# Attention heads: TensorE's last value sums and second turned score block, issued ahead of the next head's first scores

## The chip, the cores and the metric

One core of a Trainium2 chip runs the whole program. The metric is the device time of one execution in microseconds (us). Two kernels are compared by their median times; a profiled execution gives the rows below.

## The reference

Two "macaron" layers work on 1024 tokens of width 512: half feed-forward, mixer, half feed-forward. The mixer of the first layer is a Mamba2 scan, that of the second is causal attention with 32 heads of width 16 (8 key and value heads), and this case is about those heads alone:

```python
draft = einsum('bhqd,bhkd->bhqk', qr, kr) + causal
_, draft_indices = top_k(draft, 128)          # the 128 largest scores of each row stay
scores = einsum('bhqd,bhkd->bhqk', qr, kr) / sqrt(16) + mask
out = einsum('bhqk,bhkd->bhqd', softmax(scores), v)
```

A row may look at its own and earlier tokens, and of these only at its 128 best.

## The kernel before, in words

The function attention_heads_fast (L1822) takes one head after the other. The 1024 rows of a head are 8 tiles of 128; tile t has (t + 1) x 128 columns. A head goes through four phases, each in its own round of a software pipeline, so that in round n TensorE (L2063), VectorE (L2372), ScalarE (L2123) and GpSimd (L2237) work on five heads at once:

- Head n + 1: TensorE samples the scores (L1950, for a guess of each row's 128th best), then makes the scores of each tile in PSUM (scores, L1964 and L1966). VectorE takes the row maximum of tile 0 (L2270) and copies tiles 1 to 7 into z (L2274). scores(h, t) waits until VectorE has read what lay in that half of the bank before (z_done, L1959): scores(n + 1, 0) waits for the copy of tile 7 of head n.
- Heads n and n - 1: a search for the cut. ScalarE counts the scores above a trial value (L2102, four sweeps over the tiles), VectorE counts the smallest tile of two sweeps (L2307), GpSimd moves the trial value after each sweep (move, L2174) and writes the cut (L2217).
- Head n - 2: VectorE marks what reaches the cut (take, L2283). TensorE makes the scores again with the marked ones taken out (marked_scores, L1981 to L1987), VectorE finds with MAX8 which of the rest or surplus to change (pick, L2319) and writes `picked` with MATCH_REPLACE8 (L2327, named tables or picked).
- Head n - 3: the scores are made again, turned, in 12 blocks (exponents, L2013 to L2023). A block (b, t0, t1) holds 128 key tokens against the row tiles t0 to t1: blocks 0 to 3 have 512, 384, 256 and 128 columns, blocks 4 to 8 have 512, blocks 9 to 11 have 384, 256 and 128. Each lies in one of two PSUM banks by turns (ps_e). Those with b = t0 end with the mask matmul L2023. ScalarE makes the exponential of a block (L2113) into one of three buffers, TensorE sums it with the values (add_v, L2037) into ps_oT, VectorE copies and divides the sums one round later (L2335, L2342, L2344).

exponents(h, i) waits for the exponential two blocks earlier (its bank), for the row maxima and for the picks of its tiles. add_v(g) waits for the exponential of block g. ScalarE's exponentials are spread over its sweeps by a table worked out ahead (EXP_BEFORE); the last block of a head is taken at the start of the next round (LATER = 1), block 0 and block 1 in the first sweep too.

The order of TensorE is written out by hand in tables: CHUNKS_AHEAD before the sample, CHUNKS_FIRST before tile 1, and others after the marked scores or the scores of a tile. (VALUES, -1) is the last block of the head before. The core of it:

```python
CHUNKS_AHEAD = ((SCORES, 0), (VALUES, -2))
CHUNKS_FIRST = ((VALUES, -1), (SCORES, 1), (SCORES, 2))
```

Rounds run from n = -1 to 34; n + 1 is a head up to n = 30, n - 3 from n = 3.

Of the kernel before, what the change touches and what calls it, by code (L numbers as in the profile page):

```python
# [1821 lines left out]
def attention_heads_fast(nc, env, X, qT, kT, v, mixed, q_tok, k_sums):  # L1822
# [8 lines left out]
    LAST_CHUNK = [max(i for i, (b, t0, t1) in enumerate(CHUNKS) if t0 <= t < t1) for t in range(NT)]  # L1831
    SCORES, VALUES = "scores", "values"
    CHUNKS_AHEAD = ((SCORES, 0), (VALUES, -2))
    CHUNKS_FIRST = ((VALUES, -1), (SCORES, 1), (SCORES, 2))
    CHUNKS_AFTER_MARKED = {4: ((SCORES, 6), (VALUES, 4)), 7: ((SCORES, 11), (VALUES, 9))}
    CHUNKS_AFTER_SCORES = {1: ((VALUES, 0), (SCORES, 3), (VALUES, 1)), 2: ((SCORES, 4), (VALUES, 2)), 3: ((SCORES, 5), (VALUES, 3)),
                           4: ((SCORES, 7), (VALUES, 5)), 5: ((SCORES, 8), (VALUES, 6), (SCORES, 9), (VALUES, 7)),
# [16 lines left out]
    with ExitStack() as ctx:  # L1854
# [74 lines left out]
        live = lambda h: 0 <= h < AH  # L1929
# [10 lines left out]
        def _(pe):  # L1940
            def sample(h):

                if h >= 4:
                    pe.wait_ge(rows_done, h - 3)
                if h >= 6:
                    pe.wait_ge(divided, h - 5)
                if h >= 1:
                    pe.wait_ge(stats_done, 3 * h)
                for t in range(1, NT):
                    last = pe.matmul(ps_sample[:, t - 1, :], qT[:, h, t * P:(t + 1) * P], k_sums[:, h // REP, t, :],  # L1950
                                     start=t == 1, stop=True, skip_group_check=True)
                last.then_inc(sampled, 1)

            def scores(h, t):

                L, at = (t + 1) * P, z_at(t)
                done = h * NT + t - (0 < t < 4)
                if done:
                    pe.wait_ge(z_done, done)  # L1959
                for n in range(0, L, BANK):  # L1960
                    w = min(BANK, L - n)
                    diagonal = n + w == L
                    if diagonal:
                        pe.matmul(ps_z[:, at + L - P:at + L], env.ident_bf[:], env.future_bf[:], start=True, stop=False,  # L1964
                                  skip_group_check=True)
                    last = pe.matmul(ps_z[:, at + n:at + n + w], qT[:, h, t * P:(t + 1) * P], kT[:, h // REP, n:n + w],  # L1966
                                     start=not diagonal, stop=True, skip_group_check=True)
                last.then_inc(s_done, 1)

            def marked_scores(h, t):  # L1970

                L, at = (t + 1) * P, m_at(t)
                pe.wait_ge(take_done, h * W + t)
                done = h * W + t - 1 - (1 < t < 4)
                if done:
                    pe.wait_ge(pick_done, done)
                for n in range(0, L, BANK):
                    w = min(BANK, L - n)
                    diagonal = n + w == L
                    if diagonal:  # L1980
                        pe.matmul(ps_m[:, at + L - P:at + L], env.ident_bf[:], env.future_bf[:], start=True, stop=False,  # L1981
                                  skip_group_check=True)
                    pe.matmul(ps_m[:, at + n:at + n + w], qT[:, h, t * P:(t + 1) * P], kT[:, h // REP, n:n + w],  # L1983
                              start=not diagonal, stop=False, skip_group_check=True)
                for n in range(0, L, BANK):
                    w = min(BANK, L - n)
                    last = pe.matmul(ps_m[:, at + n:at + n + w], ident_taken[:], mark[:, (h * W + t) % 2, n:n + w], start=False, stop=True,  # L1987
                                     skip_group_check=True)
                last.then_inc(marked, 1)

            def turned_rows(h):

                pe.wait_ge(split_done, h + 1)
                if h + 3 < AH:
                    pe.wait_ge(stats_done, 3 * (h + 4))
                if h:
                    pe.wait_ge(rows_done, h)
                if h >= 3:
                    pe.wait_ge(divided, h - 2)
                pe.matmul(ps_rows, parts_all[:], env.ident_bf[:], start=True, stop=True).then_inc(row_done, 1)  # L2000

            def exponents(h, i):

                b, t0, t1 = CHUNKS[i]
                g = h * NCH + i
                if g >= 2:
                    pe.wait_ge(exp_done, g - 1)
                pe.wait_ge(rows_done, h + 1)
                if g == 0:
                    pe.wait_ge(set_up, FACTORS)  # L2010
                out = ps_e[g % 2]
                pe.wait_ge(pick_done, h * W + t1 - 1)
                pe.matmul(out[:, 0:t1 - t0, :], kT[:, h // REP, b * P:(b + 1) * P], qT[:, h, t0 * P:t1 * P],  # L2013
                          start=True, stop=False, skip_group_check=True)
                for t in range(t0, t1):
                    if t:
                        at = OFF[t] + b * P
                        pe.matmul(out[:, t - t0, :], picked[:, h % 2, at:at + P], ident_back[:], start=False, stop=False,  # L2018
                                  skip_group_check=True)
                    last = pe.matmul(out[:, t - t0, :], minus_rows[:, t, :], rows[:, h % 2], start=False, stop=True,  # L2020
                                     skip_group_check=True)
                if t0 == b:
                    last = pe.matmul(out[:, 0, :], env.future_bf[:], env.ident_bf[:], start=False, stop=True,  # L2023
                                     skip_group_check=True)
                last.then_inc(et_done, 1)

            def add_v(g):

                h, i = divmod(g, NCH)
                b, t0, t1 = CHUNKS[i]  # L2030
                v_at = (b * KVH + h // REP) * (AD + 1)
                pe.wait_ge(exp_done, g + 1)
                if i == 0 and h:
                    pe.wait_ge(kept_o, h)
                for t in range(t0, t1):
                    at = 2 * AD * (t % 4)
                    last = pe.matmul(ps_oT[at:at + 2 * AD, t // 4, :], env.v_all[:, v_at:v_at + 2 * AD], eT[:, g % 3, (t - t0) * P:(t - t0 + 1) * P],  # L2037
                                     start=b == 0, stop=b == t, skip_group_check=True)
                last.then_inc(av_done, 1)

            def turn_out(h):

                pe.wait_ge(kept_o, h + 1)
                if h == 0:
                    pe.wait_ge(set_up, FACTORS)
                else:
                    pe.wait_ge(divided, h)
                pe.wait_ge(rows_done, min(h + 3, AH))
                for half in range(2):
                    last = pe.matmul(ps_o[:, 4 * half:4 * half + 4, :], o_kept[:, half, :], untwist[:], start=True, stop=True,  # L2050
                                     skip_group_check=True)
                last.then_inc(o_turned, 1)

            def turn_and_add(h, steps):

                for kind, i in steps:
                    if kind == SCORES:
                        exponents(h, i)
                    elif h * NCH + i >= 0:
                        add_v(h * NCH + i)  # L2060

            pe.wait_ge(set_up, SET_UP)
            for n in range(FIRST, LAST):  # L2063
                if live(n - 3):
                    turn_and_add(n - 3, CHUNKS_AHEAD)
                if live(n + 1):
                    sample(n + 1)
                    scores(n + 1, 0)
                if live(n - 3):
                    turn_and_add(n - 3, CHUNKS_FIRST)  # L2070
                for t in range(1, NT):
                    if live(n - 2):
                        marked_scores(n - 2, t)
                        if t == ROWS_TURNED:
                            turned_rows(n - 2)
                    if live(n - 4) and t == OUT_TURNED:
                        turn_out(n - 4)
                    if live(n - 3):
                        turn_and_add(n - 3, CHUNKS_AFTER_MARKED.get(t, ()))
                    if live(n + 1):  # L2080
                        scores(n + 1, t)
                    if live(n - 3):
                        turn_and_add(n - 3, CHUNKS_AFTER_SCORES.get(t, ()))
# [455 lines left out]
```

## Time and profile before

| | |
|---|---|
| median of 3 runs | 3132.11 us (3128.52 to 3133.68) |
| profiled execution | 3127.38 us, its span 3125.6 us |
| attention heads | from 2064 to about 3004 us of the span |
| busy over the span | TensorE 89%, VectorE 80%, ScalarE 61%, GpSimd 52% |

Times in the rows are us from the start of the span. In a timeline a row has start, duration, engine, line, operation, tile written <- tile read, and in brackets how long the engine had been idle and what ended it. PE is TensorE, DVE VectorE, ACT ScalarE, POOL GpSimd. A TensorE row's duration covers the whole way of the data through the array, and the next matmul starts before it ends, so the step from start to start is what a matmul costs. Several tiles share memory and carry an older name: X is the memory of the exponentials and marks, tables that of `picked`.

### The profile page before, as it was taken

The numbers are of one execution on the slowest core, as the hardware profiler recorded it, in microseconds if no ns is written. First come the engines' busy times: TensorE is split into PE (matmuls) and PEld (weight loads), VectorE is DVE, ScalarE is ACT, GpSimd is POOL, SyncE is SP. The second block draws the span as 40 slices with busy tenths as digits, with TensorE's granted clock in tenths as the row PEclk, the third lists the DMA queues.
The fourth block names the chain that finished last, engine by engine and source line by source line (L and its number), as shares of the span: only waits on it lengthen the run. The fifth ranks groups of instructions, "written<-read, shape, count | busy, mean of one in ns | idle before, by whom it ended". The sixth has DMA issues, their size and how long they took to land. (4 is left out here: it accounts for less than half of the span.)

```text
span 3125.6 us, 50560 instructions
## 1 busy us (share of the span) xinstructions
PE 2780.4 (89%) x15833; PEld 1523.0 (49%) x15833; DVE 2494.2 (80%) x4792; ACT 1919.3 (61%) x4058; POOL 1640.1 (52%) x3595
## 2 busy tenths in 40 slices
PE   8899999999999999999999989856777777777769
PEld 4455455455455454454554554533444444444444
DVE  5678687697697696796796887768999999999846
ACT  2464554554564554554554543369999999999823
POOL 3236245255264263263362354568777787777603
PEclk9999999999999999999999999967999999998989
DMA  2223122132132242132232220000000000000010
GB/s 91 62 77 105 68 91 91 68 102 81 68 110 70 74 119 87 56 114 78 71 108 72 70 90 21 28 1 1 2 2 2 2 2 2 2 2 2 1 52 28
DMA packets 65804, 169.62 MB, mean 54 GB/s; under 512 B 11776, under 2 KB 19328, under 8 KB 64512
## 3 DMA queue, kind: packets, MB, share of 16 engines
q1 hardware_dynamic: 54448, 115.17, 11.7%
q10 hardware_dynamic: 11088, 51.19, 4.7%
q8 instruction: 131, 2.15, 0.3%
q14 instruction: 137, 1.12, 0.1%
HBM read 161.08 MB, written 5.24 MB: 53 GB/s over the span
## 5 line engine op out<-in xcount | busy, mean ns | idle before, releaser
L2102 ACT ACTIVATE X<-ah_z,ah_trial 128x512 bf16<-128x512 f32 (+6 forms) x832 | 703.9, 857 | 21.6 <-POOL ah_trial L2212 11.6
L1207 ACT ACTIVATE m_mix<-m_mix,m_cs 128x128 f32<-128x128 f32 x1024 | 312.9, 388 | 258.9 <-DMA m_mix<-cs_rows 258.9
L1089 POOL TENSOR_TENSOR m_xdec<-m_xdt,m_decay_out 128x512 f32<-128x512 f32 x112 | 142.9, 1276 | 213.0 <-DVE m_xdt L1333 202.0
L1117 POOL TENSOR_TENSOR m_squares<-m_squares 128x256 f32<-128x256 f32 x128 | 104.2, 814 | 276.0 <-ACT m_squares L1219 276.0
L1983 PE MATMUL ah_ps_m<-a_kT,a_qT 128*128 128x512 bf16 (+3 forms) x352 | 111.0, 354 | 146.8 <-DVE tables L2327 146.4
L1013 PE MATMUL m_ps_x<-m_w_out,m_gate 128*128 128x512 f32 x512 | 233.7, 599 | 0.0
L1013 PE MATMUL m_ps_d<-m_w_out,m_gate 128*128 128x512 f32 x512 | 233.5, 599 | 0.0
L2113 ACT ACTIVATE X<-ah_ps_e 128x512 f32<-128x512 f32 (+3 forms) x384 | 187.2, 488 | 59.2 <-PE ah_ps_e L2023 50.3
L2283 DVE TENSOR_SCALAR_CACHE_REDUCE X<-ah_z,ah_cut 128x256 bf16<-128x256 f32 (+6 forms) x224 | 193.6, 875 | 9.2 <-POOL ah_cut L2217 9.1
L2319 DVE MAX8 ah_top<-ah_ps_m 128x8 f32<-128x256 f32 (+6 forms) x224 | 185.5, 828 | 11.8 <-PE ah_ps_m L1987 10.8
L2274 DVE TENSOR_SCALAR_CACHE_REDUCE ah_z<-ah_ps_z 128x256 f32<-128x256 f32 (+6 forms) x224 | 182.5, 815 | 13.8 <-PE ah_ps_z L1966 13.8
L2204 POOL TENSOR_TENSOR ah_slope<-ah_between,ah_table 128x7 f32<-128x7 f32 x128 | 193.3, 1510 | 0.0
L1340 DVE TENSOR_TENSOR m_mix<-m_mix,m_cb 128x1024 f32<-128x1024 f32 x128 | 172.8, 1350 | 18.7 <-ACT m_mix L1210 18.4
L2020 PE MATMUL ah_ps_e<-ah_rows,X 128*128 128x128 bf16 x1152 | 186.5, 233 | 0.0
L2327 DVE MATCH_REPLACE8 tables<-ah_top,ah_ps_m 128x256 bf16<-128x256 f32 (+6 forms) x224 | 182.4, 814 | 0.9 <-issue 0.9
L2018 PE MATMUL ah_ps_e<-ah_ident_back,tables 128*128 128x128 bf16 x1120 | 181.7, 232 | 0.0
L1180 ACT ACTIVATE m_xbc<-m_xbc 128x1024 f32<-128x1024 f32 x80 | 84.6, 1058 | 147.5 <-DVE m_xbc L1316 147.3
L1074 POOL TENSOR_TENSOR m_xdt<-m_w_proj 128x256 f32<-128x256 f32 x32 | 24.8, 775 | 285.0 <-PE m_ps_d L887 283.8
L2102 ACT ACTIVATION_READ_ACCUMULATOR X<-ah_z,ah_trial 128x1 f32 x832 | 171.6, 206 | 0.0
L2037 PE MATMUL ah_ps_oT<-X,a_v 128*32 128x128 f32 x2304 | 168.3, 300 | 3.0 <-DVE ah_o_kept L2335 2.9
L1316 DVE SCALAR_TENSOR_TENSOR m_xbc<-m_b_tok,m_conv_p,m_xbc 128x1023 f32<-128x1023 f32 (+2 forms) x96 | 129.4, 1348 | 44.6 <-ACT m_xbc L1172 42.4
L887 PE MATMUL m_ps_y<-hT,m_w_proj 128*128 128x512 f32 x320 | 153.6, 603 | 5.3 <-ACT m_gate L1152 3.3
(328 smaller groups left out, 7517.7 us busy)
## 6 DMA issues: line engine op xcount, KB each, us to landing
m_mix<-cs_rows SPq DMA_DIRECT2D x128, 512.0 KB, 4.5
m_w_proj<-in_w_proj ACTq DMA_DIRECT2D x69, 512.0 KB, 3.3
m_fade<-fade_rows SPq DMA_DIRECT2D x224, 128.0 KB, 3.0
m_w_out<-in_w_out ACTq DMA_DIRECT2D x7, 2048.0 KB, 8.0
X<-in_x SPq DMA_DIRECT2D x8, 256.0 KB, 4.6
m_w_out<-in_w_out SPq DMA_DIRECT2D x1, 2048.0 KB, 10.1
x_away<-X SPq DMA_DIRECT2D x1, 2048.0 KB, 7.3
X<-x_away SPq DMA_DIRECT2D x8, 256.0 KB, 6.1
```

What stands on the lines that cost most here:

```text
L1013: last = pe.matmul(ps_out[c % 2], gate[:, half * 4 + i, c * P:(c + 1) * P], w_out[:, half * 4 + i, :], start=(half == 0 and i == 0), stop= ...
L1207: act.activation(mix[:, u % 3, h, :], mix[:, u % 3, h, :], ACT.Relu, bias=cs[:, c, h0 + h:h0 + h + 1], scale=-1.0).then_inc(lag_done, 1)
L1340: dve.tensor_tensor(mix[:, u % 3], mix[:, u % 3], cb[:, c, :].unsqueeze(1).to_broadcast([P, HU, P]), ALU.mult).then_inc(mix_done, 1)
L2018: pe.matmul(out[:, t - t0, :], picked[:, h % 2, at:at + P], ident_back[:], start=False, stop=False, skip_group_check=True)
L2020: last = pe.matmul(out[:, t - t0, :], minus_rows[:, t, :], rows[:, h % 2], start=False, stop=True, skip_group_check=True)
L2102: act.activation(sign[:, at % 2, 0:(t + 1) * P], z[:, h % RING, cols(t)], ACT.Sign, bias=trial[:, h % RING, 0, t - 1:t], scale=-1.0, accum ...
L2113: act.activation(eT[:, g % 3, 0:w * P], ps_e[g % 2][:, 0:w, :].rearrange("p b q -> p (b q)"), ACT.Exp, scale=0.25).then_inc(exp_done, 1)
L2204: pool.tensor_tensor(slope[:, 0], between[:, 1], table[:, 5], ALU.pow).then_inc(own, 1)
L2274: dve.tensor_scalar(z[:, h % RING, cols(t)], ps_z[:, z_at(t):z_at(t) + (t + 1) * P], 0.0, NEG, ALU.add, ALU.max, accum_out=row_max[:, h % ...
L2283: dve.tensor_scalar(mark[:, (h * W + t) % 2, 0:(t + 1) * P], z[:, h % RING, cols(t)], cut[:, h % 2, t - 1:t], 0.0, ALU.is_ge, ALU.add, acc ...
L2319: dve.max(top[:, r], ps_m[:, m_at(t):m_at(t) + (t + 1) * P]).then_inc(pick_step, 1)
L2327: dve.match_replace(picked[:, h % 2, cols(t)], top[:, r], ps_m[:, m_at(t):m_at(t) + (t + 1) * P], TAKEN).then_inc(pick_done, 1)
```

## The change

The tables of TensorE's order are split: what stood behind the scores of tile 0 of the next head is now partly ahead of them. Before, a round began: block 0, value sums of the last block but one, sample, scores(n + 1, 0), value sums of the last block, block 1, block 2. Now: block 0, value sums of the last block but one, sample, value sums of the last block, block 1, scores(n + 1, 0), block 2. Nothing else is changed, and no other engine's order.

```diff
-    CHUNKS_FIRST = ((VALUES, -1), (SCORES, 1), (SCORES, 2))
+    CHUNKS_FIRST = ((VALUES, -1), (SCORES, 1))
+    CHUNKS_AFTER_FIRST = ((SCORES, 2),)
...
                 if live(n + 1):
                     sample(n + 1)
+                if live(n - 3):
+                    turn_and_add(n - 3, CHUNKS_FIRST)
+                if live(n + 1):
                     scores(n + 1, 0)
                 if live(n - 3):
-                    turn_and_add(n - 3, CHUNKS_FIRST)
+                    turn_and_add(n - 3, CHUNKS_AFTER_FIRST)
```

## Rows read from the trace of the kernel before

**Rows 1.** Busy time by stretch: stretch, length, each engine's us, granted clock, DMA.
```profile
2200.00:2400.00 200.00, 152.94 (x1642) 93.21 (x1639) 193.90 (x549) 192.93 (x473) 157.18 (x560) 0.94 0.01 2
2400.00:2600.00 200.00, 153.80 (x1647) 94.89 (x1645) 195.03 (x542) 194.37 (x478) 159.80 (x564) 0.94 0.01 2
```

**Rows 2.** VectorE, 2200 to 2800: its wait for another engine; L2270 with idle before.
```profile
DVE ah_top L2319 <- PE ah_ps_m L1987: 0.7, 1, 0.7
...
L2270 DVE TENSOR_REDUCE ah_row_max<-ah_ps_z 128x1 f32<-128x128 f32 x22 | 6.4, 292 | 2.7
```

**Rows 3.** Waits of ScalarE and TensorE, 2200 to 2800: us in total, times, longest.
```profile
ACT X L2113 <- PE ah_ps_e L2023: 18.9, 24, 1.2
...
PE ah_ps_m L1983 <- DVE tables L2327: 101.3, 88, 2.7
PE ah_ps_z L1964 <- DVE ah_z L2274: 36.6, 22, 2.0
```

**Rows 4.** Timeline of TensorE, one round, and a block of 384 columns at full clock.
```profile
2409.25 0.34 PE L2013 MATMUL ah_ps_e<-a_qT,a_kT 128*128 128x384 bf16 x1
...
2409.91 0.42 PE L2037 MATMUL ah_ps_oT<-X,a_v 128*32 128x128 f32 x8
...
2416.26 0.22 PE L2023 MATMUL ah_ps_e<-ident_bf,future_bf 128*128 128x128 bf16 x1
...
2418.36 0.34 PE L1950 MATMUL ah_ps_x<-a_k_sums,a_qT 128*128 128x17 bf16 x7
2420.73 0.23 PE L1964 MATMUL ah_ps_z<-future_bf,ident_bf 128*128 128x128 bf16 x1 [2.04 <-DVE ah_z L2274]
...
2420.95 0.41 PE L2037 MATMUL ah_ps_oT<-X,a_v 128*32 128x128 f32 x2
2421.29 0.50 PE L2013 MATMUL ah_ps_e<-a_qT,a_kT 128*128 128x384 bf16 x1
...
2422.33 0.42 PE L2013 MATMUL ah_ps_e<-a_qT,a_kT 128*128 128x256 bf16 x1
```

**Rows 5.** Timeline of VectorE, the same round and the end of the next.
```profile
2420.59 0.08 DVE L2274 DVE_READ_ACCUMULATOR ah_z<-ah_ps_z 128x1 f32 x1
...
2421.05 0.29 DVE L2270 TENSOR_REDUCE ah_row_max<-ah_ps_z 128x1 f32<-128x128 f32 x1
...
2447.76 0.08 DVE L2274 DVE_READ_ACCUMULATOR ah_z<-ah_ps_z 128x1 f32 x1
```

**Rows 6.** Timeline of ScalarE, exponentials of the last block, block 0, block 1.
```profile
2417.27 0.29 ACT L2113 ACTIVATE X<-ah_ps_e 128x128 f32<-128x128 f32 x1
...
2418.94 0.61 ACT L2113 ACTIVATE X<-ah_ps_e 128x512 f32<-128x512 f32 x1
...
2422.58 0.49 ACT L2113 ACTIVATE X<-ah_ps_e 128x384 f32<-128x384 f32 x1 [1.08 <-PE ah_ps_e L2023]
```

**Rows 7.** Timeline of TensorE: the three shortest gaps before scores(n + 1, 0).
```profile
2173.41 0.23 PE L1964 MATMUL ah_ps_z<-future_bf,ident_bf 128*128 128x128 bf16 x1 [0.37 <-DVE ah_z L2274]
...
2200.84 0.23 PE L1964 MATMUL ah_ps_z<-future_bf,ident_bf 128*128 128x128 bf16 x1 [0.44 <-DVE ah_z L2274]
...
2886.28 0.23 PE L1964 MATMUL ah_ps_z<-future_bf,ident_bf 128*128 128x128 bf16 x1 [0.21 <-DVE ah_z L2274]
```

**Rows 8.** VectorE's first instruction of each head (line L2257), 2200 to 2840.
```profile
L2257 DVE COPY ah_stats<-ah_ps_x x24: 159/160/165, 2200.7 to 2829.8; 128x7 f32<-128x7 f32 x24
```

**Rows 9.** Stretches with a low granted clock, and VectorE's MAX8 beside such stretches.
```profile
2223.20:2226.60 3.40, 3.40 (x18) 1.51 (x18) 2.61 (x6) 2.54 (x8) 2.17 (x11) 0.51 0.00 0
2420.70:2424.70 4.00, 3.97 (x32) 2.62 (x33) 3.72 (x19) 2.92 (x8) 2.12 (x12) 0.57 0.00 0
2414.46:2417.88 3.42, 2.71 (x27) 1.60 (x27) 3.30 (x7) 3.42 (x9) 1.31 (x8) 1.00 0.00 0
...
2225.14 1.23 DVE L2319 MAX8 ah_top<-ah_ps_m 128x8 f32<-128x1024 f32 x1 [0.70 <-PE ah_ps_m L1987]
...
2151.59 0.57 DVE L2319 MAX8 ah_top<-ah_ps_m 128x8 f32<-128x384 f32 x1 [0.78 <-PE ah_ps_m L1987]
```

## Prediction

> **What bounds the kernel now.** The change touches one stage only, the attention heads, so the first view is the busy time by stretch. In the middle of that stage VectorE is busy 195 us of 200 and ScalarE 194, while TensorE is busy 154 [rows 1]. Two engines are nearly full, and the question is which of them sets the pace. The waits of VectorE answer it: over 600 us, 22 heads, it waited 0.7 us in all for another engine [rows 2]. Its other idle time (4.5 us of 200, so 0.6 us per head) lies between its own dependent instructions. One short wait per head is too short for the view of waits: the row maximum of tile 0 (L2270) stood idle 2.7 us over 22 heads, 0.12 each [rows 2], for the scores of tile 0.
>
> ScalarE does wait for another engine: 18.9 us over the same 600 us, 24 times, 0.86 us per head, all before an exponential and all for a block of turned scores that ends with the mask matmul L2023 [rows 3]. TensorE waits most: 101.3 us for the picks of VectorE, and 36.6 us before the scores of tile 0 (L1964), 22 times, for VectorE's copy of the last tile of scores (L2274) [rows 3].
>
> One head shows how these hang together. The sample of TensorE (L1950) starts at 2418.36 and lasts 0.34. The next thing in its order is scores(n+1, 0), which must wait until VectorE has read the last accumulator of tile 7 at 2420.67; it starts at 2420.73. Only then come the last value sums (L2037, 2420.95) and turned block 1 (2421.29 to 2422.33) [rows 4, 5]. ScalarE wants block 1 at 2421.50 and gets it 1.08 us later [rows 6]. So the ScalarE wait is real, and the change aims straight at it. But the chain that sets the period goes through VectorE: last copy of tile 7, scores of tile 0, row maximum, all of the next head's VectorE work, last copy again, 27.17 us later [rows 5].
>
> **The change, part by part.** It adds and removes no instruction, no wait and no DMA. On TensorE it moves three matmul groups (two L2037 matmuls, and block 1 with its seven short matmuls behind one of 384 columns) from behind scores(n+1, 0) to ahead of it. They pass no other queue; SP and GpSimd have nothing here. It acts only where both n+1 and n-3 are heads, in 28 of the 36 rounds; in the rounds before and after the order is as before.
>
> 1. *What the moved work waits for.* Both groups wait for the exponential of the previous head's last block, and for picks that are long done. That exponential (128 columns) starts at 2417.27 and takes 0.29, over 1.1 us before TensorE is through with the sample at 2418.70 [rows 4, 6]. No new wait: 0.
>
> 2. *Whether it fits.* The moved work takes 0.34 for the value sums (2420.95 to 2421.29), and block 1 takes 0.66 at full clock by its twin of the same size (2409.25 to 2409.91), 1.04 at the low clock [rows 4]. So 1.00 us, or 1.4 with the block at the low clock, in a gap that is 36.6 / 22 = 1.66 us on average [rows 3]. Behind the delayed scores stands VectorE's row maximum, and so the whole bound chain; every 0.1 us of overrun in each head would be 2.8 us. In usual heads there is none. Three heads have short gaps, 0.37, 0.44 and 0.21 us [rows 7]: there scores(n+1, 0) comes 0.63, 0.56 and 0.79 us later. Term: +2.0 us, between 0 (if TensorE is no longer late in those heads) and 3.
>
> 3. *What ScalarE gains.* The wait for block 1 goes: 0.86 us per head. It is worth nothing by itself, since VectorE did not wait for ScalarE or for the cuts that hang on it [rows 2]. What is late next: ScalarE can move ahead only until it wants the last block of the previous head sooner than TensorE has it. The last matmul of that block starts at 2416.26 and ends at 2416.48, ScalarE takes it at 2417.27, so 0.8 us of lead is all there is, and from the second or third head on ScalarE should wait there (a 128-column exponential) for about as long as it did at block 1 [rows 4, 6]. Term: 0; at the end of the stage a lead of 0.8 us could survive, so between -1 and 0.
>
> 4. *What VectorE gains.* It starts its heads 27.35 us apart on average (629.1 us for 23 of them), and the undisturbed one of rows 5 takes 27.17 [rows 5, 8]. A part of these 0.18 us is TensorE being late at its low clock: in the 4 us behind scores(n+1, 0) the granted clock is 0.57, which is mostly the 1.2 GHz level [rows 9]. TensorE had stood idle for 2.04 us just before it fell [rows 4]. With the gap half filled, the clock may not fall there, and block 1 is out of the way. Bounds: 0 to 0.18 x 23 - 0.7 = 3.4 us (0.7 is the one disturbed head of rows 9). I take 1.2, nearer to nothing, because the one wait of a usual head that can be named (0.12 before L2270) stays: those scores are still released by the same copy. Term: -1.2.
>
> The Trainium skill ("TensorE: Matmul & The Clock Gate", section on the second failure mode, psum-queue cycling) says that short idle gaps between matmul groups make the clock swing and that each swing costs throughput. By that rule alone, filling a gap can only help, and the sum would be term 4 at its full -3.4. The trace agrees that the clock falls behind such gaps, but VectorE hides nearly all of what that costs.
>
> Sum: 2.0 - 1.2 = +0.8 us. The profiled execution took 3127.4 us (span 3125.6), so it would take 3128.2. It lies 4.7 us under the median of the three runs, 3132.1, so the median would be about 3133. What a measurement of this kernel can tell from no change is about 0.2%, 6.3 us; the forecast is no measurable change.
>
> **The rivals.**
>
> *A, the forecast: ScalarE's wait moves, VectorE's period stays.* 3127 to 3139. For it: 0.7 us of VectorE waits in 600 [rows 2]. Against it: nothing in the rows, except that the clock's pattern is not fixed.
>
> *B, slower: the low clock moves onto the marked scores of tile 7.* The low stretch comes about once a head and now lies where VectorE has enough to do. If the gap before scores(n+1, 0) no longer brings it there, it may fall after another long gap (those before marked scores reach 2.7 us [rows 3]), the one ahead of tile 7, whose marked scores VectorE's MAX8 needs at once. The trace has such a head: granted clock 0.51 from 2223.2 on, and MAX8 waited 0.70 us; a MAX8 of 384 columns waited 0.78 in an early head [rows 9]. At 0.70 us in all 28 heads that is +19.6 us, 3152; in 12 heads +8.4, 3141. It decides from 9 heads on (9 x 0.70 = 6.3). Against it: that gap is there already, and in the head of rows 4 the clock stayed at 1.00 behind it (2414.46 to 2417.88) [rows 9]. For it: after such a delay the heads stand differently to the clock, so it would come in some heads and not in all.
>
> *C, faster: ScalarE was the bound after all.* Then its 0.86 us come off each of 28 heads: -24 us, 3108. The profile speaks clearly against it. A mixed case, in which a third of the wait counts, gives -8 us, 3124.
>
> *D: the moved work runs at the low clock in each head.* Then 0.54 for the value sums (an estimate, scaled as the block: 0.34 x 1.04 / 0.66) and 1.04 give 1.58 us against a gap of 1.66: it just fits, with 0 to 0.1 us of delay, 0 to 3 us in all, 3136. It counts as no change.
>
> **How the numbers follow.** A 0.68, B 0.19, C with its mixed case 0.07, D 0.06. Faster by over 0.2%: C, 0.07. Slower: nearly all of B and a little of the top of A, 0.19. The rest, 0.74, is within 0.2%. The range takes A and D whole, the runs' own spread of 5 us, and the lower half of B: 3125 to 3143.
>
> **What the next profile would show.** Step 1 right: no wait of the L2037 pair for ScalarE. Step 2: the idle before L1964 falls from 1.66 to about 0.7 us in a usual head, and L2270 waits no longer than 0.12. Step 3: the wait of L2113 keeps its total of near 19 us over 22 heads but stands before the 128-column exponential; POOL's waits for ScalarE fall a little. Step 4: heads 27.2 to 27.3 us apart. Wrong, towards B: MAX8 (L2319) with waits of over 5 us on L1987, and a low clock ahead of tile 7. Wrong, towards C: heads under 27.0 us apart, and VectorE instructions that are fewer us in sum than before.

## The result and the profile after

The changed kernel takes 3143.5 us (median of 7 runs, 3139.2 to 3145.4) against 3130.9 us for the kernel before in the same series: a ratio of 1.0039 with a 95% interval of 1.003 to 1.0049. It is slower by 12.6 us, which is more than the 0.2% that the prediction took as the bound of no change, and half a microsecond above its range (3125 to 3143).

The profiled execution has a span of 3142.1 us against 3125.6. Between VectorE's first instruction of head 4 and that of head 31, 27 heads, it needs 753.2 us (2148.3 to 2901.5); before it needed 740.7 (2145.4 to 2886.1). So 12.4 of the 16.5 us lie there, 0.46 us per head (27.90 against 27.43). Another 2.9 us are there already at the first head (2069.7 against 2066.7), in code that is the same in both, and 1.2 us come after head 31. The medians differ by 12.6, about what the heads alone give. The head's start is in what follows always this first instruction (before, then after):

```profile
L2257 DVE COPY ah_stats<-ah_ps_x x28: 158/160/165, 2145.4 to 2886.1; 128x7 f32<-128x7 f32 x28
```

```profile
L2261 DVE COPY ah_stats<-ah_ps_x x28: 158/160/168, 2148.3 to 2901.5; 128x7 f32<-128x7 f32 x28
```

The busy time by stretch, the columns as in [rows 1]: VectorE and ScalarE have each lost 3 to 4 us of busy time in 200, and TensorE 3 to 5.

```profile
2200.00:2400.00 200.00, 150.36 (x1594) 92.29 (x1609) 190.95 (x529) 189.91 (x464) 156.13 (x554) 0.93 0.01 2
2400.00:2600.00 200.00, 148.38 (x1573) 90.55 (x1595) 190.86 (x536) 190.17 (x468) 155.10 (x552) 0.93 0.01 2
```

The waits of VectorE, ScalarE and TensorE from 2200 to 2800 (us in total, times, longest), which answer to [rows 2, 3]. The change adds four lines, so L2323 is the L2319 of before (MAX8), L2274 the L2270 (row maximum), L2117 the L2113 (exponential), and on TensorE L1965, L1982 and L1984 are the L1964, L1981 and L1983 of before:

```profile
DVE ah_top L2323 <- PE ah_ps_m L1988: 7.8, 18, 0.8
DVE ah_row_max L2274 <- PE ah_ps_z L1967: 4.7, 8, 0.8
...
ACT X L2117 <- PE ah_ps_e L2024: 14.9, 20, 1.3
ACT ah_rows L2125 <- PE ah_ps_x L2001: 14.2, 13, 1.3
...
PE ah_ps_m L1984 <- DVE tables L2331: 82.9, 63, 2.7
PE ah_ps_m L1982 <- DVE X L2287: 34.7, 22, 1.6
...
PE ah_ps_z L1965 <- DVE ah_z L2278: 7.8, 12, 0.7
```

VectorE, which had waited 0.7 us for TensorE, now waits 12.5. That is the loss: the 22 heads from head 6 to head 28 take 614.0 us (2203.2 to 2817.2) where they took 601.8 (2200.7 to 2802.5), 12.2 us more, and VectorE's waits grew by 11.8. The last three rows show where TensorE's idle time went: the 36.6 us before scores(n + 1, 0) shrank to 7.8, and 34.7 us appeared before the marked scores of tile 1 (1.58 per head). The work moved ahead filled one gap and left another of the same size behind it, since those marked scores cannot start before VectorE has marked tile 1.

Three places of the timelines show what VectorE waits for. First TensorE in one round, behind the new gap; the low clock is seen in the durations (0.31 instead of 0.22 for 128 columns, 0.53 instead of 0.33 for 384):

```profile
2482.53 0.23 PE L1965 MATMUL ah_ps_z<-future_bf,ident_bf 128*128 128x128 bf16 x1 [0.73 <-DVE ah_z L2278]
...
2484.78 0.23 PE L1982 MATMUL ah_ps_m<-future_bf,ident_bf 128*128 128x128 bf16 x1 [1.58 <-DVE X L2287]
...
2487.43 0.29 PE L1982 MATMUL ah_ps_m<-future_bf,ident_bf 128*128 128x128 bf16 x1
2487.51 0.53 PE L1984 MATMUL ah_ps_m<-a_kT,a_qT 128*128 128x384 bf16 x1
2487.83 0.53 PE L1988 MATMUL ah_ps_m<-X,ah_ident_taken 128*128 128x384 bf16 x1
```

The MAX8 of tile 2 (128x384) stands waiting for just these, and the granted clock of the stretch is at the lower of its two levels, 1.2 GHz (VectorE's timeline, then the row by stretch):

```profile
2488.46 0.57 DVE L2323 MAX8 ah_top<-ah_ps_m 128x8 f32<-128x384 f32 x1 [0.59 <-PE ah_ps_m L1988]
```

```profile
2486.20:2489.20 3.00, 2.78 (x21) 1.53 (x19) 2.38 (x11) 1.73 (x5) 2.81 (x8) 0.50 0.00 0
```

Second, the marked scores of tile 7, near the end of an earlier round, with MAX8 behind them (TensorE, VectorE, then the row by stretch):

```profile
2420.96 0.59 PE L1984 MATMUL ah_ps_m<-a_kT,a_qT 128*128 128x512 bf16 x1 [2.45 <-DVE tables L2331]
```

```profile
2423.04 1.23 DVE L2323 MAX8 ah_top<-ah_ps_m 128x8 f32<-128x1024 f32 x1 [0.78 <-PE ah_ps_m L1988]
```

```profile
2420.90:2424.30 3.40, 3.34 (x17) 1.42 (x18) 2.56 (x5) 2.41 (x8) 2.10 (x11) 0.51 0.01 2
```

Third, the very end of a round. Here the low stretch covers block 0 and the value sums behind it, and ends just ahead of the sample; the moved work starts only at 2370.20, at about the time when VectorE is done with tile 7 (2370.42), and the scores of tile 0 follow 0.9 us later. The row maximum waits 0.74 us (the row by stretch, TensorE's timeline, VectorE's):

```profile
2366.40:2370.50 4.10, 4.10 (x34) 2.10 (x31) 3.96 (x9) 2.95 (x9) 3.77 (x14) 0.59 0.00 0
```

```profile
2370.20 0.41 PE L2038 MATMUL ah_ps_oT<-X,a_v 128*32 128x128 f32 x2
2370.54 0.34 PE L2014 MATMUL ah_ps_e<-a_qT,a_kT 128*128 128x384 bf16 x1
...
2371.10 0.22 PE L1965 MATMUL ah_ps_z<-future_bf,ident_bf 128*128 128x128 bf16 x1
```

```profile
2371.41 0.29 DVE L2274 TENSOR_REDUCE ah_row_max<-ah_ps_z 128x1 f32<-128x128 f32 x1 [0.74 <-PE ah_ps_z L1967]
```

In the kernel before, 21 of the 22 rounds from 2229 to 2830 had their low stretch right behind scores(n + 1, 0), from about 1 to 4.5 us after the head's start, and VectorE did not wait there. After, none of them has it there, and the low stretch wanders: behind the marked scores of tile 1 (between 3.4 and 7.9 us), at tile 7 (22 to 26 us) or over the end of the round (up to 27.4 us), with waits of VectorE at each place, though not in each round (heads 8, 9 and 25 have the low stretch and no wait). Of the 7.8 us of MAX8 waits, 3.6 stand before tile 2 (10 times), 3.9 before tile 7 (7 times) and 0.3 before tile 3.

### The profile page after: what moved, and what is told of

Read it like the earlier page. It is cut to its first block and busy times, and to the rows that moved or that the text cites. A ratio compares the mean times of both kernels' runs of the same rounds, so it can differ in the third digit from the quotient of the medians.

```text
span 3142.1 us, 50449 instructions
## 1 busy us (share of the span) xinstructions
PE 2772.4 (88%) x15722; PEld 1523.6 (48%) x15833; DVE 2490.8 (79%) x4792; ACT 1921.6 (61%) x4058; POOL 1641.0 (52%) x3595
## 5 line engine op out<-in xcount | busy, mean ns | idle before, releaser
L2117 ACT ACTIVATE X<-ah_ps_e 128x512 f32<-128x512 f32 (+3 forms) x384 | 187.4, 489 | 54.6 <-PE ah_ps_e L2024 44.2
L1984 PE MATMUL ah_ps_m<-a_kT,a_qT 128*128 128x512 bf16 (+3 forms) x318 | 103.8, 358 | 122.2 <-DVE tables L2331 122.0
L2323 DVE MAX8 ah_top<-ah_ps_m 128x8 f32<-128x256 f32 (+6 forms) x224 | 185.5, 828 | 17.9 <-PE ah_ps_m L1988 16.7
```

Source lines behind the costliest of these rows:

```text
L2117: act.activation(eT[:, g % 3, 0:w * P], ps_e[g % 2][:, 0:w, :].rearrange("p b q -> p (b q)"), ACT.Exp, scale=0.25).then_inc(exp_done, 1)
L2323: dve.max(top[:, r], ps_m[:, m_at(t):m_at(t) + (t + 1) * P]).then_inc(pick_step, 1)
```

## The experiments

Two theories were left after this. **Overrun**: work ahead of scores(n + 1, 0) delays them whenever TensorE is late, and the row maximum with them. **Gap**, later **clock**: the place of TensorE's idle time decides where its low clock falls, and the loss is what VectorE waits for there. Each run was compared with the kernel before on the same chip.

### Half the change each

```diff
-    CHUNKS_FIRST = ((VALUES, -1), (SCORES, 1))
-    CHUNKS_AFTER_FIRST = ((SCORES, 2),)
+    CHUNKS_FIRST = ((VALUES, -1),)
+    CHUNKS_AFTER_FIRST = ((SCORES, 1), (SCORES, 2))
```

> Only the last value sums (0.34 us of TensorE) stand ahead of scores(n+1, 0); block 1 stays behind it. Gap theory (the time is lost where TensorE's idle time, moved from before scores(n+1, 0) to before the marked scores of tile 1, brings the low clock onto the marked scores of tiles 2 and 7): the idle time is now shared, some 1.3 us before scores(n+1, 0) and under 1 us before tile 1, MAX8 waits under 3 us in 600, and the time is that of before, 3127 to 3135. Overrun theory (the time is lost because work ahead of scores(n+1, 0) delays it whenever TensorE is late): a third of the work moved, a third of the loss, 3133 to 3136, with waits at L2270 (row maximum).

Measured: 3134.7 us against 3131.6, ratio 1.0010 (1.0001 to 1.0019), within both ranges.

```diff
-    CHUNKS_FIRST = ((VALUES, -1), (SCORES, 1))
-    CHUNKS_AFTER_FIRST = ((SCORES, 2),)
+    CHUNKS_FIRST = ((SCORES, 1),)
+    CHUNKS_AFTER_FIRST = ((VALUES, -1), (SCORES, 2))
```

> Only block 1 (0.66 us at full clock) stands ahead of scores(n+1, 0); the value sums stay behind it. Gap theory: about 1.0 us idle before scores(n+1, 0), 1.3 before tile 1; the low clock sits after one or the other, 3131 to 3140. Overrun theory: two thirds of the loss, 3137 to 3141, waits at L2270 in the heads in which TensorE is late. Both: ScalarE no longer waits before block 1's exponential.

Measured: 3140.3 us, ratio 1.0030 (1.0018 to 1.0042), within the overrun theory's range and 0.3 us above the other.

By the times alone the overrun theory had the better of it: a quarter of the loss (3.1 us) for a third of the work, 0.7 of it (8.7 us) for two thirds. But its waits are only a part of the loss. VectorE's waits from 2200 to 2800, value sums alone, then block 1 alone:

```profile
DVE ah_top L2323 <- PE ah_ps_m L1988: 3.7, 7, 0.8
DVE ah_row_max L2274 <- PE ah_ps_z L1967: 1.7, 9, 0.2
```

```profile
DVE ah_top L2323 <- PE ah_ps_m L1988: 4.7, 10, 0.8
DVE ah_row_max L2274 <- PE ah_ps_z L1967: 3.9, 13, 0.3
```

The larger part is MAX8, which no delay of scores(n + 1, 0) explains. The waits of the row maximum do grow with the work ahead of it: up to 0.2 us with the value sums, up to 0.3 with block 1, up to 0.8 with both. But they stand only in rounds that begin within some 2 us after a low stretch has ended. The gap theory's own numbers for the first run were missed as well: MAX8 waits 3.7 us and not under 3, and TensorE's idle time before scores(n + 1, 0), expected at 1.3 us in each head, was 5.4 us in 7 of them, because the low stretch lay over the end of most rounds and used it up.

### Dummy work in one gap

The changed order with TensorE kept busy before tile 1:

```diff
+            def fill(h, count):
+                for _ in range(count):
+                    pe.matmul(ps_z[:, BANK:2 * BANK], qT[:, h, P:2 * P], kT[:, h // REP, 0:BANK], start=True, stop=True,
+                              skip_group_check=True)
...
                     turn_and_add(n - 3, CHUNKS_AFTER_FIRST)
+                if live(n - 3) and live(n + 1):
+                    fill(n + 1, 5)
```

> The changed order, with five matmuls of 512 columns whose result nobody reads (1.1 us at full clock) in the idle time before the marked scores of tile 1. Gap theory: no low clock from 4 to 8 us after the head's start, the MAX8 waits of 384 columns go; with them at least half of the 12 us: 3131 to 3137, and 3128 or less if the low clock at tile 7 goes too. Overrun theory: more work for TensorE changes nothing before scores(n+1, 0), 3141 to 3147.

Measured: 3144.3 us, ratio 1.0045 (1.0031 to 1.0059), within the overrun theory's range. Nothing was won. The low clock did leave tile 2, as expected, but went to tiles 4 and 5 (10 to 15 us after the head's start) and to tile 7, where MAX8 waits 0.2 to 0.8 us as well (8.3 us in 16 waits; the row maximum waits 4.9 us, as in the changed kernel). The gap theory was right on the place and wrong on the gain: it had taken for granted that a low stretch that is driven away is gone.

The old order with dummies in front of scores(n + 1, 0):

```diff
                     sample(n + 1)
+                    if live(n - 3):
+                        fill_block(n - 3, 1, 5)
                     scores(n + 1, 0)
...
+            def fill_block(h, i, count):
+                g = h * NCH + i
+                if g >= 2:
+                    pe.wait_ge(exp_done, g - 1)
+                for _ in range(count):
+                    pe.matmul(ps_e[g % 2][:], kT[:, h // REP, 0:P], qT[:, h, 0:BANK], start=True, stop=True,
+                              skip_group_check=True)
```

> The old order, with five matmuls of 512 columns whose result nobody reads (1.1 us at full clock) ahead of scores(n+1, 0), as long as the moved work, while the real work stays behind. Gap theory: both gaps are short, the low clock behind scores(n+1, 0) goes, MAX8 hardly waits; 3126 to 3134. Overrun theory: dummy work in that place costs what the moved work costs, 3139 to 3146, with waits at L2270.

Measured: 3148.3 us, ratio 1.0053 (1.0039 to 1.0067). This is more than the change itself costs, with the old order. The waits of VectorE, 2200 to 2800:

```profile
DVE ah_top L2336 <- PE ah_ps_m L1987: 8.5, 17, 0.8
DVE ah_row_max L2287 <- PE ah_ps_z L1966: 6.2, 10, 0.9
DVE ah_z L2291 <- PE ah_ps_z L1966: 2.0, 5, 0.5
```

The gap theory as written (idle time has to move to before tile 1) is wrong by this run, in which 12.8 us of idle time stand before tile 1 in 22 rounds and not 34.7. The overrun theory got its number, but 8.5 of the 16.7 us of these waits are MAX8's again, at tiles 5 and 7. What both runs had in common: the gap before scores(n + 1, 0) was filled, in part or wholly, and the low clock then came somewhere else (in the run with dummies before tile 1 through the moved work). Hence the clock theory: some gap always brings the low clock while three are open, and the one before scores(n + 1, 0) is the one behind which it does no harm.

### Every gap filled, in both orders

Dummies of 256 columns into spare columns of the bank of the value sums, whose tile is made twice as wide for it (before tile 1, in the changed order, of 512 columns into the second half of ps_z). They shorten the gaps and do not close them: before tiles 4 and 7 up to 1.2 us are left.

```diff
+            FILL = {0: 10, 4: 8, 7: 14}
+            def fill(n, place):
+                for _ in range(FILL.get(place, 0) if live(n - 3) and live(n + 1) else 0):
+                    pe.matmul(ps_oT4[:, 2:4, :], env.ident_bf[:], kT[:, 0, 0:2 * P], start=False, stop=True,
+                              skip_group_check=True)
...
                     sample(n + 1)
+                    fill(n, 0)
                     scores(n + 1, 0)
...
                 for t in range(1, NT):
+                    fill(n, t)
```

> The old order with matmuls that nobody reads (256 columns each, 0.11 us at full clock) in all three long gaps of a round: 10 before scores(n+1, 0), 8 before the marked scores of tile 4, 14 before those of tile 7, so that TensorE is nearly always busy. Clock theory (some gap always brings the low clock; in the old order it is the gap before scores(n+1, 0), behind which nobody needs TensorE, and any work put there sends the low clock to tiles 5 to 7, the sample and tile 0, where VectorE waits): with all gaps filled it comes nowhere, heads are 27.2 us apart, 3122 to 3129. Overrun theory (work ahead of scores(n+1, 0) delays it, whatever the clock): as the run with five dummies, 3140 to 3150.

Measured: 3125.3 us against 3131.7, ratio 0.9979 (0.997 to 0.9988).

The changed order with FILL = {0: 3, 1: 4, 4: 8, 7: 14}:

> The changed order with its gaps filled in the same way (3 before scores(n+1, 0), four of 512 columns before the marked scores of tile 1, 8 before tile 4, 14 before tile 7). Clock theory: the order by itself costs nothing once the clock stays up, so the same time as the old order filled, 3122 to 3130. Overrun theory: the loss stays, 3140 to 3147.

Measured: 3125.4 us, ratio 0.9979 (0.997 to 0.9988).

The overrun theory fails in both. The old order has 1.1 us of dummies ahead of scores(n + 1, 0) here, as in the run before, and the row maximum does not wait once; so work ahead of these scores costs something only together with the low clock. The two orders are equal: 6 us below the kernel before, some 18 below the changed kernel without dummies. By stretch the granted clock is at its full level all through (the old order, then the changed one):

```profile
2400.00:2600.00 200.00, 171.28 (x1888) 108.79 (x1886) 195.01 (x541) 194.34 (x477) 159.56 (x567) 1.00 0.01 2
```

```profile
2400.00:2600.00 200.00, 171.61 (x1864) 106.27 (x1862) 194.99 (x542) 195.42 (x480) 160.24 (x568) 1.00 0.01 2
```

Heads 4 to 31 are 27.25 and 27.24 us apart, where it was 27.43 and 27.90 before:

```profile
L2268 DVE COPY ah_stats<-ah_ps_x x28: 158/160/164, 2146.7 to 2882.5; 128x7 f32<-128x7 f32 x28
```

```profile
L2276 DVE COPY ah_stats<-ah_ps_x x28: 159/160/165, 2146.4 to 2881.9; 128x7 f32<-128x7 f32 x28
```

The view of waits has no wait of VectorE for another engine in 600 us. Of the 5.0 us that the old order gains over these 27 heads in the profiles, 4.1 come from five (4, 5, 6, 29 and 30) in which the low stretch of the kernel before stood elsewhere. The 22 heads between them took 600.8 us (2229.0 to 2829.8) with the low stretch behind scores(n + 1, 0) in 21, and take 599.8 (2228.0 to 2827.8) without it: at that place it cost about 1 us in all. The waits of ScalarE, old order and changed order, show that the change did what it says, and what that is worth:

```profile
ACT X L2124 <- PE ah_ps_e L2024: 17.2, 22, 1.0
```

```profile
ACT ah_rows L2140 <- PE ah_ps_x L2002: 11.9, 22, 0.6
ACT X L2132 <- PE ah_ps_e L2025: 1.3, 4, 0.4
```

ScalarE's wait before block 1 is gone, it takes block 1 1.1 us earlier in the round (0.35 us after the head's start and not 1.46) and meets another wait, before row_out (L2140), and the time is the same to 0.1 us.

### The same dummies in both orders, the gap before scores(n + 1, 0) left alone

The old order with FILL = {4: 8, 7: 14}:

> The old order with dummies only before tiles 4 and 7; the gap before scores(n+1, 0) stays empty. Clock theory: the low clock stays in its harmless place behind scores(n+1, 0) in every head, also in those two or three in which the old kernel had it elsewhere; no loss against before, 3124 to 3132. Were the sum of idle time what counts, the clock would be up everywhere here too. Overrun theory: no change, 3128 to 3134.

Measured: 3129.1 us against 3131.7, ratio 0.9994 (0.9985 to 1.0003): within both ranges, and no difference from the kernel before that is clear of noise.

The changed order with the same FILL:

> The changed order with dummies only before tiles 4 and 7 (8 and 14 of 256 columns), the twin of the old order's run with the same dummies. Clock theory: the low clock leaves tile 7 and tiles 5 and 6, and the changed order comes to the time of its twin or a little above, 3125 to 3132. Overrun theory: what is ahead of scores(n+1, 0) is unchanged, so the loss stays, 3140 to 3147.

Measured: 3141.7 us against 3131.2, ratio 1.0035 (1.0024 to 1.0045).

In this pair the dummies are the same, and the order alone makes 12 to 13 us. The overrun theory's range held in both, the clock theory's in the old order only, and neither saw what happens. In the old order the gap before scores(n + 1, 0) is open, 39.1 us in 22 rounds, and the clock stays up in 17 of the 22 all the same; my expectation that it would fall there in every head was wrong:

```profile
PE ah_ps_z L1965 <- DVE ah_z L2285: 39.1, 22, 2.1
```

In the changed order (waits of VectorE and TensorE, then the row by stretch):

```profile
DVE ah_top L2338 <- PE ah_ps_m L1989: 11.7, 26, 0.7
...
PE ah_ps_m L1983 <- DVE X L2302: 34.7, 22, 1.6
...
PE ah_ps_z L1966 <- DVE ah_z L2293: 16.3, 22, 1.0
```

```profile
2400.00:2600.00 200.00, 172.30 (x1752) 106.44 (x1751) 189.93 (x529) 188.91 (x462) 155.85 (x551) 0.91 0.01 2
```

There is no wait of the row maximum in it at all, so the overrun theory has nothing to explain the loss with, although its number came out. What is left are the gap before tile 1, 1.58 us in every round, and the one before scores(n + 1, 0), 0.74 us on average, just ahead of it. The low stretch begins at them or up to some 2 us behind them in every single round (1.6 to 4.3 us after the head's start, ending between 5.8 and 9.7), on the marked scores of tiles 2 and 3. One such round:

```profile
2536.30 0.23 PE L1966 MATMUL ah_ps_z<-future_bf,ident_bf 128*128 128x128 bf16 x1 [0.73 <-DVE ah_z L2293]
...
2538.55 0.29 PE L1983 MATMUL ah_ps_m<-future_bf,ident_bf 128*128 128x128 bf16 x1 [1.58 <-DVE X L2302]
```

```profile
2537.80:2544.60 6.80, 6.05 (x44) 3.30 (x45) 6.12 (x25) 5.28 (x16) 5.72 (x22) 0.50 0.00 0
```

My clock theory expected that filling tiles 4 and 7 would bring the changed order down to its twin, and missed that these gaps at the start of the round suffice. TensorE's idle time there is about the same in both orders (39.1 us in one gap, and 16.3 and 34.7 us in two); why the clock falls in every round of the one and in few of the other is not shown.

### Dummies in the first and last rounds too

The old order, all gaps filled, with `if live(n - 2) or live(n - 3)` in place of `if live(n - 3) and live(n + 1)`.

> The old order, all three gaps filled, and the same dummies also in the rounds at the start and the end of the stage (n = 2 and n = 31 to 34). Clock theory: one to three us less than with the middle rounds alone, 3121 to 3126, from MAX8 waits at the start and the end. Rival: there VectorE waits for cuts and TensorE's own work, and the dummies change nothing or cost a little, 3124 to 3129.

Measured: 3126.5 us against 3131.2, ratio 0.9983 (0.9974 to 0.9991), not below the run with the middle rounds alone: above the clock theory's range, within the rival's. The one 1.22 us wait of MAX8 at the start fell to 0.33, but the row maximum there waited 0.84 instead of 0.23.

## Why the prediction was wrong

**What the loss is made of.** Over the 22 heads from head 6 to head 28 the time follows VectorE's waits for TensorE in every run:

| run | 22 heads, us | VectorE's waits in them, us |
|---|---|---|
| old order, all gaps filled | 600.2 | 0 |
| kernel before | 601.8 | 0.7 |
| old order, tiles 4 and 7 filled | 602.6 | 1.4 |
| value sums ahead | 606.8 | 6.3 |
| block 1 ahead | 608.4 | 8.6 |
| the change | 614.0 | 12.5 |
| the change, tiles 4 and 7 filled | 614.1 | 11.7 |
| the change, dummies before tile 1 | 616.7 | 14.7 |
| old order, five dummies before scores(n + 1, 0) | 618.6 | 16.9 |

These waits are there only where the clock falls: at full clock (all gaps filled) neither order has one in these heads.

**Right: what bounds the stage.** VectorE sets the pace, and ScalarE's wait is worth nothing. With the gaps filled, both orders run at about 27.2 us per head, near the 27.17 of [rows 5], and moving 17 us of ScalarE's waits to other places, with 4 us less in all, changed the time by 0.1 us.

**Right in part: step 1 and step 3.** The moved work hardly waited for ScalarE (0.7 us in 600, for a value sum), and ScalarE's wait moved on to other instructions. At full clock it went mostly to row_out and not to the last block; step 3 had not followed that chain. In the changed kernel itself ScalarE waits longer than before and not the same 19 us: 29.1 us, of which 14.2 before row_out, 8.4 before block 0 and 6.6 before the last block. One reading is off by a little: VectorE's idle time is 5.0 us of 200 by the row shown (195.03 busy), so 0.7 us per head, and not 4.5 and 0.6.

**Step 2: the term was about right in two of its three heads and wrong in its sentence "In usual heads there is none."** The two early heads paid about as worked out (the row maximum waited 0.76 and 0.75 us, where 0.63 and 0.56 were expected), head 31 did not. But in 8 of the 22 rounds from 2200 to 2800 the low clock had covered the end of the round before, and there the moved work overruns: 4.7 us of waits where 0.12 a head was expected. Rival D had priced the moved work at the low clock, but not block 0 and the value sums ahead of it at the low clock, which use up the gap before the moved work starts.

**Step 4: this is the step that failed.** It said that with the gap half filled the clock may not fall there, and counted only what would be gained (-1.2 us). The clock indeed no longer fell there. It fell elsewhere, and cost 12.5 us of VectorE waits in 22 rounds: 7.8 before MAX8 and, through step 2, 4.7 before the row maximum. There was hardly anything to gain either: the low stretch behind scores(n + 1, 0) cost about 1 us in 22 rounds, 0.05 us per head of the 0.18 that the step had as its upper bound. The step asked what the filled gap would do and not where the idle time goes: VectorE sets TensorE's pace, so idle time that is filled at one place stands at the next, here before the marked scores of tile 1, which wait for VectorE's marks. The question "what is late next" was put for ScalarE and left out for TensorE.

**Rival B had the mechanism, with a chance of 0.19,** and its price per hit was somewhat high (0.70; measured 0.2 to 0.8, on average 0.43 over 18 hits and 0.56 at tile 7). It looked for one place, tile 7; MAX8 waits there made 3.9 us of 12.5. Tile 2, which had the 0.78 us row in [rows 9], made 3.6, and the row maximum 4.7. The argument against it, that the gap before tile 7 had been there all along with the clock up, was the fault: in the kernel before the clock was up at tile 7 together with a low stretch at a harmless place in nearly every round. In two of the rounds in which it was elsewhere, at 2223 and at 2841, a head took 28.3 and 28.2 us (27.5 and 27.5 in the old order with all gaps filled), and that was in the trace. The measured 12.6 us lie between B's +8.4 for 12 heads and +19.6 for 28, in part by luck: over a third of VectorE's waits are the row maximum's, which B did not have.

**The rule of the Trainium skill** ("TensorE: Matmul & The Clock Gate", section "A second HAM failure mode: psum-queue depth-cycling") says that frequent short idle times between groups of matmuls make the clock swing and cost throughput. The prediction read it as saying that filling a gap can only help. With all long gaps filled the runs agree with the rule: granted clock 1.00 and -6.4 us. With one gap filled they contradict the prediction's reading of it: +12.6 us with real work, +16.6 with dummies.

**Open.** It is shown that the waits come with the low stretches; what decides where a low stretch falls is not. Why the clock stays up in most rounds of the old order with tiles 4 and 7 filled, while a gap of the same length before scores(n + 1, 0) is open, was not tested. Nor was it tried to fill the gaps with real work in place of dummies.

## What to carry to other kernels

Before you fill an idle gap of an engine that another one paces, write down where the idle time stands afterwards, and who waits for the work behind it. A low clock in every round is not a cost until someone waits for TensorE during it; find out where it stands, and count as a risk every edit that may move it. Here it went from every round only with all long gaps shortened together, and then the order no longer mattered; with the gap before scores(n + 1, 0) left open it went from 17 of 22 rounds.

## What the runs showed of the hardware that was not expected

- Useless matmuls made the kernel a little faster: 32 of them per round, 28 rounds, 3125.3 us against 3131.7. TensorE was busy 171 us of 200 instead of 154, and the granted clock rose from 0.94 to 1.00.
- With dummies before tiles 4 and 7, a gap of 1.6 us before tile 1 behind one of 0.7 us before scores(n + 1, 0) came with the low clock in every round; a single gap of 1.8 us on average before scores(n + 1, 0) came with it in 5 rounds of 22.
- The place of the low stretch drifts from round to round and comes back: in the changed kernel the heads take 27.5, 27.6, 27.7, 28.0, 28.3, 28.2 us and then 27.5 again (2567 to 2762), and the low stretch comes earlier each time before it jumps back.
